# Layer 0 of a four-layer image network: matmuls without use while TensorE waits at three places

## The reference

```
xn   = group norm of x                            (32 groups of 6 channels)
h    = layer norm of the tokens of xn over the 192 channels
x_in, z = split(h @ w_up + b_up)                  (384 channels each)
x_act   = silu(causal 4-tap convolution of x_in over the tokens)
q, k, v = x_act @ w_q, x_act @ w_k, x_in
mLSTM scan over the 1024 tokens, 12 heads of 32, with gates from (q, k, v)
out  = (norm of the scan + skip * x_act) * silu(z) @ w_down
y    = (xn, silu(xn @ w_lin) and out, added) -> 3x3 convolution 192 -> 192
x    = x + a batch norm of y over all 16 images
```

## Time and profile before

| | |
|---|---|
| time, median of 3 runs | 8747.54 us (8743.06 to 8752.52) |
| the profiled execution: its own time / its span | 8753.26 us / 8751.5 us |
| mean granted TensorE clock | 0.899 of full speed |
| TensorE matmuls | 7433.0 us (85%), 35246 instructions |
| VectorE | 5686.3 us (65%) |
| ScalarE | 3834.1 us (44%) |
| GpSimd | 2230.9 us (25%) |
| layer 0 | from 0 to about 3400 us of the span, mean clock 0.93 |

### The profile page before, as it was taken

One profiled execution on the slowest core, in us unless ns is written; L12 is line 12 of the kernel. 1 busy time (PEld: TensorE's weight loads), 2 busy tenths in 40 slices (PEclk: granted clock), 3 DMA queues, 4 the chain that ended last, 5 costly groups with the idle time before them and its releaser, 6 DMA issues.

```text
span 8751.5 us, 96151 instructions
## 1 busy us (share of the span) xinstructions
PE 7433.0 (85%) x35246; PEld 3527.2 (40%) x35246; DVE 5686.3 (65%) x9661; ACT 3834.1 (44%) x7430; POOL 2230.9 (25%) x1862
## 2 busy tenths in 40 slices
PE   7998989999898985668888888888888888888867
PEld 4544444444445553123333433433333333343343
DVE  4666665666666664458667667766866766766774
ACT  4444444444445442444543543543444354354320
POOL 1222222222222221003412421431341242143152
PEclk9899999999999996779999898999989899989988
DMA  1111111111111112015444543554544445455375
GB/s 63 37 38 37 37 37 37 37 42 37 37 40 44 40 40 83 0 52 149 154 130 118 164 143 98 172 150 112 161 157 125 123 154 144 107 166 152 107 220 140
DMA packets 244214, 849.78 MB, mean 97 GB/s; under 512 B 46413, under 2 KB 49177, under 8 KB 243361
## 3 DMA queue, kind: packets, MB, share of 16 engines
q1 hardware_dynamic: 150272, 388.71, 16.6%
q0 software_dynamic: 92160, 453.06, 16.4%
q10 hardware_dynamic: 1312, 1.87, 0.1%
HBM read 602.10 MB, written 89.68 MB: 79 GB/s over the span
## 4 chain that ended last, share of the span: by engine, by line
PE 36%; DVE 15%; DMA 4%; ACT 4%; issue 3%; POOL 1%; SPq 1%; DVEq 0%; ACTq 0%; POOLq 0%
PE ps L2203 7%; PE ps L2648 5%; PE ps L2433 4%; DVE arena L1904 4%; PE ps L2192 3%; PE ps L2659 2%; PE ps L2629 2%; DMA arena<-img,arena 2%; PE ps L2131 2%; PE ps L2319 2%; PE ps L2117 2%; SPq L2682 1%; DVE arena L403 1%; DMA arena<-arena 1%; POOL arena L2466 1%
## 5 line engine op out<-in xcount | busy, mean ns | idle before, releaser
L2466 POOL DMA_INDIRECT arena<-img,arena x1152 | 1379.5, 1197 | 2566.5 <-DMA img<-arena 1812.5
L2363 DVE SCALAR_TENSOR_TENSOR arena<-arena 128x384 f32<-128x384 f32 x1152 | 752.3, 653 | 634.8 <-DMA arena<-img,arena 630.0
L1904 DVE TENSOR_REDUCE arena<-ps 128x2 f32<-128x1024 f32 x768 | 894.5, 1216 | 324.6 <-PE ps L2172 321.8
L2059 ACT ACTIVATE arena<-ps 128x512 f32<-128x512 f32 x1536 | 821.8, 600 | 280.8 <-PE ps L2192 274.6
L985 POOL TENSOR_TENSOR arena<-arena 128x512 f32<-128x512 f32 x384 | 443.0, 1160 | 1951.0 <-DMA arena<-decay 1951.0
L2648 PE MATMUL ps<-arena 128*64 128x512 f32 x3072 | 818.5, 659 | 127.1 <-DMA arena<-arena 72.8
L2203 PE MATMUL ps<-arena 128*64 128x512 f32 x3072 | 869.6, 649 | 0.0
L2433 PE MATMUL ps<-arena 128*96 128x128 f32 x4608 | 636.9, 298 | 93.4 <-DVE arena L2352 93.2
L2433 PEld LDWEIGHTS ps<-arena 128*96 128x96 f32 x4608 | 584.0, 180 | 289.7 <-issue 289.2
L1118 DVE TENSOR_TENSOR arena<-ps,arena 128x512 f32<-128x512 f32 x384 | 265.4, 691 | 504.6 <-issue 270.0
L952 PE MATMUL ps<-arena 128*128 128x512 f32 x1152 | 507.2, 596 | 0.0
(11 more groups left out here) (344 smaller groups left out, 12091.3 us busy)
## 6 DMA issues: line engine op xcount, KB each, us to landing
arena<-arena SPq DMA_DIRECT2D x1024, 144.5 KB, 2.9
arena<-decay SPq DMA_DIRECT2D x384, 256.0 KB, 3.3
img<-arena SPq DMA_DIRECT2D x162, 384.0 KB, 2.6
arena<-img,arena POOLq DMA_INDIRECT x1152, 4.7
arena<-y SPq DMA_DIRECT2D x16, 768.0 KB, 6.4
arena<-x SPq DMA_DIRECT2D x16, 768.0 KB, 6.3
out<-arena SPq DMA_DIRECT2D x16, 768.0 KB
arena<-x SPq DMA_DIRECT2D x16, 512.0 KB, 5.2
```

The source lines that it names most:

```text
L1904: dve.tensor_reduce(out, self.wides[B.at("max", b, g, n, h) // 2].rearrange("p (a b) -> p a b", a=2), AX.X, AL.max).then_inc(*S.mark("max_ ...
L2059: act.activation(self.p[n % 6], B("score", b, n)[:, :], ACT.Exp).then_inc(*S.mark("p_act", b, n))
L2363: dve.scalar_tensor_tensor(gb[:, 0:384], gb[:, 384:768], pp[:, 1, n:n + 1], gb[:, 0:384], AL.mult, AL.add).then_inc(*S.mark("corner_x", b, n))
L2466: pool.indirect_dma_start(self.g[n % 6], None, img, bass.IndirectOffsetOnAxis(ap=ii[:, n:n + 1], axis=0)).then_inc(*S.landed(f"{self.tag}g ...
```

## The change

A helper issues `n` matmuls of 256 columns into a bank: weights are the constant matrix `ONE`, moving data a slice of the weights `WQ`. Both are in SBUF from the start. Nobody reads the product; each place then overwrites the bank with `start=True`. It is called 6 times over at the means, 3 at the first scores of an image, 6 at the convolution. At the convolution the wait for `parts lower` moves behind the waits for the first pair of banks, so that the helper stands before it.

```diff
+    def pe_spin(self, pe, ps, n):
+        for _ in range(n):
+            pe.matmul(ps[:, 0:256], self.C["ONE"], self.W["WQ"][:, 0, 0:256], start=True, stop=True)
@@ pe_layer
             mean.append(ps)
+        self.pe_spin(pe, mean[0], 6)
         pe.wait_ge(*S("gn0_dve", b, "out", 1))
@@ pe_chunks
                 pe.wait_ge(*free)
+                if n == 0:
+                    self.pe_spin(pe, ps, 3)
                 pe.wait_ge(*S("qd", b, n))
@@ pe_conv
         pe.wait_ge(*S("prep0", "u", 1, 3))
-        pe.wait_ge(*S("parts", b, "lower"))
         for n in range(3):
             banks = []
             for q, by in enumerate(("first", "y")):
                 ps, free = B.hold(("conv", b, n, q), ("conv_dve", b, n, by))
                 pe.wait_ge(*free)
                 banks.append(ps)
+            if n == 0:
+                self.pe_spin(pe, banks[0], 6)
+                pe.wait_ge(*S("parts", b, "lower"))
```

## The result

| | before | after |
|---|---|---|
| median of 5 runs | 8749.42 us (8743.06 to 8752.52) | 8692.62 us (four of them 8671.25 to 8694.08) |
| ratio | | 0.9928, 95% interval 0.9913 to 0.9942 |
| profiled execution: its time / span | 8753.26 / 8751.5 us | 8690.50 / 8688.7 us |
| mean granted clock | 0.899 | 0.911 |
| last matmul of layer 0 starts at | 3383.3 us of the span | 3303.4 us |

The kernel is 0.7% faster, 57 us by the medians and 63 us from span to span. One of the five executions of the changed kernel took 15971.14 us, for a reason that no trace shows, and is left out of the ratio. I forecast 76 less, 8671, in a range of 8622 to 8722. Layer 0 itself became 79.9 us shorter; 17 us of it aren't in the total, because layers 1 to 3 took longer in this execution. Experiments c1 and c2 ask whether that belongs to the change.

A forecast was written before the change was run, and what follows sets the result against it. TensorE was taken to bound layer 0, losing time in waits and at the halved clock behind them. Convolution 15, means 38, first image -3 and scores 26 sum to 76 us saved, median 8671 us, range 8622 to 8722.

The forecast's parts named there:

- What bounds layer 0: Layer 0: TensorE is the busiest engine, 85% of the span, and loses time by waits and the low clock behind them.
- whether the time is kept: Layer 0: the other engines wait for TensorE after each place, so all shifts as one and the saving stays.
- The convolution: Wait for L1357, 15 images: six calls end 0.60 us late, full clock saves 1.59; 1.0 us an image, 15 us.
- The means: Wait for L498, 15 images: calls end 0.39 us late, full clock returns 2.9; 2.5 us an image, 38 us.
- The first scores: 16 images: between a loss of 1.6 and a gain of 2.84 us each; 1.6 taken, 26 us.
- the scores give all: Rival at the first scores: clock stays up all the way, 16 x 2.84 = 45 us, total 8652; chance 0.18.
- The first image: Means of the first image: clock already low, six calls take 6.0 us against a 3.27 us wait, 2.7 us late once.
- Weight loads: Rival at all three places: loads aren't hidden, a record costs 0.454 us, nothing is left, about 8755; chance 0.05.
- Clock not held: Rival at all places: useless matmuls don't hold the clock, only the delays remain, 21 us, 8769; chance 0.06.
- another engine: Rival: GpSimd or ScalarE is as late as TensorE, whose waits grow by what is saved; no change, 8747; chance 0.06.

The follow-up runs named there:

- c1: The kernel before, profiled again with no edit: 9001.43 us against 9024.13 for other runs of the same program, ratio 0.9991.
- c2: The changed kernel, profiled again with no edit next to the kernel before: 8965.47 us, ratio 0.9937.
- e5: e4 plus five useless calls in the joining of the branches, behind the wait for its first bank: 8917.66 us, ratio 0.9894 to the kernel before.
- e3: The changed kernel with only the six calls at the means kept: 9014.80 us, ratio 1.0007 to the kernel before.
- e7: The changed kernel without its calls at the means: one execution, layer 0 ends at 3301.1 us, the changed kernel's at 3303.4 and 3306.1.
- e4: The changed kernel with the means' six calls moved between the two banks' waits, into the first bank: 8917.36 us, ratio 0.9894 to the kernel before.
- e6: e5 plus six calls ahead of the last part of the convolution, in the wait at L1417: 8894.15 us, ratio 0.986 to the kernel before.
- e9: The changed kernel with calls at the convolution alone, three instead of six: one execution, the place takes 9.27 us, against 9.37 with six.
- e10: e6 without the calls in the joining of the branches: 8638.28 us against 8742.66 for the kernel before, ratio 0.988.
- e1: The changed kernel with only the three calls at the first scores kept: 8986.91 us against 8996.56 for the kernel before, ratio 0.9978.

## Why the prediction was right in sum and wrong in a step

**What bounds layer 0, and whether the time is kept: right.** The periods show it: 206.65 to 201.87 us an image. Of the 4.78 us, 1.56 come from the convolution, 3.08 from the scores and 0.44 from the means; the scan between scores and means gives 0.93 back, and the rest, 0.6, lies elsewhere. No other engine took over at the change's three places: TensorE's wait at L1281 is 34.8 us in 14 waits before and 34.7 in 14 after, at L939 it is 0.8 us each time in both. In e5 one did, at a fourth.

**The convolution: right in mechanism, mis-sized, 1.0 us forecast, 1.56 measured.** The term that was too large is the price of a useless record: 0.265 us from the convolution's own records, 0.224 measured, so six calls end 0.07 us after the input and not 0.60. The convolution's records change weights and the helper's don't. That differs by 0.04 us; I didn't test whether it is the reason.

**The means: wrong.** The step that failed is that the calls start as soon as the matmul before them ends, which the prediction took for granted there: "Wait 2.81 against 3.2 us: 0.39 late". I had looked up who empties the banks at the convolution and the scores, but not here. The second bank is emptied by L1122 of the scan, which stands directly before L498 on VectorE. The trace of before had it (timeline of VectorE):

```profile
1628.36 0.55 DVE L1122 TENSOR_TENSOR arena<-ps,arena 128x384 f32<-128x384 f32 x1
1628.83 1.26 DVE L498 TENSOR_SCALAR arena<-arena 128x1024 f32<-128x1024 f32 x2
```

TensorE was idle from 1627.65; the bank came at 1628.9. 2.5 us an image forecast; measured 0.44 in the first pair of traces, -0.09 in c1 and c2, nothing in e3, and in e7 the place is even 0.6 to 0.85 us shorter without the calls. e4 shows the cause by moving the calls alone: 6.44 us. The lateness costs some 1.3 us, since the five images of the changed kernel whose late calls ran at full clock take 7.6 to 7.8 us; the low clock in the other nine costs 1.9 us more.

**The first scores: right in mechanism, mis-sized.** 1.6 us forecast, 3.1 measured; it is the rival "the scores give all" (2.84). I had priced in that the clock would fall in the two waits left open. It stayed up in 14 of 16 images, and six records took 1.40 us. By the rule of the Trainium skill's page "TensorE: Matmul & The Clock Gate" (Part 4, PE-mode transpose), that transposes don't count as busy as other matmuls do, the clock would have fallen more often here, right behind six transposes. The trace has two such images of 16, in which the six records take 2.7 us; no run tests the rule by itself. Part of the saving is lost further on: in every kernel with these calls, and no wait filled at L1417, the scan to the means takes 46.1 to 46.5 us, against 45.3 to 45.7 without. There the clock now stays down for two stretches behind the wait for L1417 (0.50 and 0.53 above) where it was one (kernel before, same image, columns as above):

```profile
1622.80:1626.19 3.39, 3.39 (x16) 2.11 (x14) 0.00 (x0) 0.93 (x3) 0.22 (x1) 0.50 0.56 175
1626.21:1629.61 3.40, 1.44 (x11) 1.09 (x9) 1.85 (x4) 1.93 (x6) 0.85 (x1) 1.00 0.02 7
```

Why the moments lie so is open. That the low clock is what the scan loses by is shown by e6, which fills that wait and has 43.8.

**The first image: wrong sign, small.** 2.7 us late forecast; its first scores came at 140.5 instead of 141.6 us (140.1 instead of 141.8 in c2 and c1). Its twelve records took 4.69 us, 0.39 each. That is the low clock by their length; the granted clock reads 1.00 that early in the trace, so no reading confirms it. The time behind them was shorter.

**Weight loads.** The rule of the Trainium skill's page "TensorE: Matmul & The Clock Gate" (Part 3, "What overlaps and what doesn't"), that a weight load overlaps a running matmul only if the row groups differ, would have made a record 0.454 us here. It was 0.224, with 0.190 us for its load, so this rival falls and the measurement stands against the rule.

**Clock not held, another engine:** both fall, the first by the stretches at 1.00 behind the calls.

**The size of the total.** By place the forecast had 15 (convolution), 38 (means), -3 (first image) and 26 (scores). Summed over all images, the first pair of traces has 23.5, 8, 1 and 49, less 13.5 given back in the scan: 68 of the 80 us, the other 12 in stretches that the change doesn't touch. c1 and c2 have 24, 3, 2, 49 and -14, together 64 of 68. That the sum came out is luck: the means were priced 30 to 35 us too high, the scores 23 and the convolution 9 too low, the forecast had no term for what the scan gives back, and the two pairs scatter by 12 us. Had only the means been as measured, the same sum would have given 41 to 46.

## What to carry to other kernels

Useless matmuls paid here where they started with the wait and work at the low clock stood behind it; filling half of a 2.6 us wait was enough. Ask first what the useless work itself must wait for: its bank has to be empty when the idle time begins, not when the input comes, and too many or too late calls stand between a ready input and its use (3.3 us here). Then ask which engine is late next: at the fourth place all that the clock gave was a longer wait for VectorE.

## What the runs showed of the hardware

- At the convolution, 2.2 to 2.7 us of idleness were followed by a stretch at 1.2 GHz in all 15 images of the kernel before (of before and of c1); with 0.76 to 1.1 us of it left, in none of e9's.
- Twelve f32 records of 128 x 256 with the same 128 x 128 weights: 2.69 us at 2.4 GHz, 4.35 us where the clock was down for most of it.
- Layers 1 to 3, with the gathers by indirect DMA, took 5354 to 5385 us in six profiled executions (before, after, e7 to e10) and 5611 to 5682 us in eight others (c1, c2, e1 to e6), with the same code for these layers. The gathers' own busy time hardly differs (1380 us in before, 1394 in c1), but GpSimd waits 751 us for VectorE before them in c1 and 510 in before. The cause is open.
